# A fused two-layer kernel: 77 context rows without padding in the first attention, and its transposes in pairs

## The reference, cut to what matters

```
xn = layernorm(x)
c2s = softmax((xn Wq_c + bq_c)(ctx Wk_s + bk_s)^T / 16) (ctx Wv_s + bv_s)      # [B, 1024, 256]
s2c = softmax((ctx Wq_s + bq_s)(xn Wk_c + bk_c)^T / 16) (xn Wv_c + bv_c)       # [B,   77, 256]
s2c = interpolate 77 rows linearly to 1024
gate = sigmoid([c2s, s2c] Wg^T + bg)
x = x + tanh(g) * (gate * c2s + (1 - gate) * s2c)
```

## Time and profile before

| | |
|---|---|
| time of three runs | 1067.16, 1067.27, 1069.19 us; median 1067.27 |
| the profiled execution | 1068.09 us, of which the span from first to last instruction is 1066.3 |
| PE busy | 1019.4 us, 96% of the span |
| DVE, ACT, POOL busy | 506.3, 478.4, 305.4 us |
| mean granted clock of PE | 0.986 of full |
| the chain that ended last | PE 83%, DVE 7%, ACT 5% |
| most of the span | MLP products at L1022, 55% of the chain |

### The profile page before, as it was taken

The page is one execution under the profiler, slowest core; times in us unless marked ns, Lnnn a source line. Parts: engine busy times, 40 slices in busy tenths (PEclk is TensorE's granted clock), DMA queues, the critical chain, the costliest instruction groups (busy, mean ns, idle before and its releaser), DMA issues.

```text
span 1066.3 us, 14394 instructions
## 1 busy us (share of the span) xinstructions
PE 1019.4 (96%) x5218; PEld 828.4 (78%) x5218; DVE 506.3 (47%) x1391; ACT 478.4 (45%) x877; POOL 305.4 (29%) x432
## 2 busy tenths in 40 slices
PE   7989998997999999999999999999999999999996
PEld 4757776766789987887889877878898788788885
DVE  6567766765633362456333625563246345134311
ACT  1345442554545353445544544455445444534431
POOL 0025453321251244223502442235034322112111
PEclk9989999998999999999999999999999999999998
DMA  9930003631376365443664654337546545344440
GB/s 336 376 112 2 1 1 119 200 119 40 110 243 206 131 214 158 127 126 113 227 212 138 198 158 137 121 114 233 201 151 197 160 125 158 102 136 153 144 138 23
DMA packets 44276, 158.93 MB, mean 149 GB/s; under 512 B 6448, under 2 KB 6832, under 8 KB 43306
## 3 DMA queue, kind: packets, MB, share of 16 engines
q0 software_dynamic: 29952, 104.88, 31.8%
q1 hardware_dynamic: 10826, 40.63, 11.1%
q10 hardware_dynamic: 3424, 12.45, 3.0%
HBM read 138.01 MB, written 29.36 MB: 157 GB/s over the span
## 4 chain that ended last, share of the span: by engine, by line
PE 83%; DVE 7%; ACT 5%; issue 2%; POOL 1%; DMA 0%; DVEq 0%; POOLq 0%; ACTq 0%
PE psum L1022 55%; PE psum L918 3%; PE psum L822 2%; PE psum L1094 2%; PE psum L1096 2%; PE psum L1095 2%; PE psum L1070 1%; PE psum L832 1%; PE psum L704 1%; PE psum L680 1%; PE psum L944 1%; PE psum L926 1%; PE psum L718 1%; PE psum L734 1%; PE psum L1048 1%
## 5 line engine op out<-in xcount | busy, mean ns | idle before, releaser
L2249 POOL DMA_DIRECT2D mlp_pieces<-in_mlp x176 | 96.5, 556 | 432.9 <-PE psum L1022 429.4
L1022 PE MATMUL psum<-hidden_a_high,mlp_pieces 128*128 128x512 f32 x512 | 205.7, 402 | 0.0
L1022 PE MATMUL psum<-hidden_b_high,mlp_pieces 128*128 128x512 f32 x512 | 202.9, 396 | 0.0
L1022 PE MATMUL psum<-hidden_b_low,mlp_pieces 128*128 128x512 f32 x512 | 199.6, 390 | 0.0
L1022 PE MATMUL psum<-hidden_a_low,mlp_pieces 128*128 128x512 f32 x512 | 199.6, 390 | 0.0
L2095 DVE TENSOR_TENSOR hidden_a_low<-hidden_a,hidden_a_high 128x512 fp32r<-128x512 f32 x128 | 88.2, 689 | 174.0 <-ACT hidden_a_high L1484 173.1
L2095 DVE TENSOR_TENSOR hidden_b_low<-hidden_b,hidden_b_high 128x512 fp32r<-128x512 f32 x64 | 44.4, 693 | 169.4 <-ACT hidden_b_high L1484 169.4
L1022 PEld LDWEIGHTS psum<-hidden_a_high,mlp_pieces 128*128 128x128 f32 x512 | 96.1, 188 | 23.5 <-issue 2.8
L1501 ACT ACTIVATE hidden_a<-psum,mlp_scales 128x512 f32<-128x512 f32 x64 | 44.1, 689 | 154.4 <-PE psum L1022 154.4
L1022 PEld LDWEIGHTS psum<-hidden_a_low,mlp_pieces 128*128 128x128 f32 x512 | 96.2, 188 | 21.7 <-issue 2.6
L1022 PEld LDWEIGHTS psum<-hidden_b_high,mlp_pieces 128*128 128x128 f32 x512 | 96.2, 188 | 20.2 <-issue 0.8
(11 more groups left out here) (290 smaller groups left out, 1825.4 us busy)
## 6 DMA issues: line engine op xcount, KB each, us to landing
mlp_pieces<-in_mlp POOLq DMA_DIRECT2D x176, 512.0 KB, 4.0
slots<-in_zeros SPq DMA_DIRECT2D x3, 3072.0 KB, 37.0
yrows<-expert_rows ACTq DMA_DIRECT2D x18, 512.0 KB, 3.1
mlp_piece_to_examine<-in_mlp SPq DMA_DIRECT2D x16, 512.0 KB, 4.4
slot_rows<-slots SPq DMA_DIRECT2D x15, 512.0 KB, 4.6
x_residual<-in_x SPq DMA_DIRECT2D x4, 1024.0 KB, 23.4
out<-x_residual SPq DMA_DIRECT2D x8, 512.0 KB, 3.4
expert_in<-in_Wi SPq DMA_DIRECT2D x1, 2048.0 KB, 15.6
```

The source lines that it names most:

```text
L1022: last = mm(o, a, b, start=(k == 0 and i == 0), stop=(k == n_k - 1 and i == len(parts) - 1))
L2249: pool.dma_start(mlp_ring[:, r % RING, :], d["mlp"][r % NCHECK]).then_inc(ring_in[r % RING], 16)
```

## The change

Three things. First, `LP` is gone: the arrays have L = 77 partitions, each of the mixing's products contracts over 77 rows, all seven memsets and every wait on `zero_ready` are removed (so is POOL's wait for the last expert product). Second, the transposes of the next batch are issued as pairs of tiles in more places: before the loop after experts 5 and 6; in the loop one pair before `a_sub2char`, one after it, one after `a_sum(5)`, one after `a_sum(6)`. ACT's copies are placed to match, ahead of or behind its own `a_sub2char` copy; DVE's `a_start` is cut in two, with `a_sub2char` between the halves. Third, `kept_context` moves from behind expert 7 to behind expert 2 in DVE's list.

The declaration of VVl below stands for nine such ones.

```diff
-LP = 96
...
-        VVl = place("weights", "values_and_gate_low", [LP, B, 2 * D], F32R)
+        VVl = place("weights", "values_and_gate_low", [L, B, 2 * D], F32R)
...
@@ PE, a_sum
-                mm(ps[:, first, :], P1Th[:, t], VVh[:, b, :], start=True, stop=False)
+                mm(ps[:, first, :], P1Th[0:L, t], VVh[0:L, b, :], start=True, stop=False)
...
@@ PE
             for e in range(5, E):
                 expert(e)
-            a_turn(1, range(JT))
+                if e < E - 1:
+                    a_turn(1, (2 * e - 10, 2 * e - 9))
+            a_turn(1, range(4, JT))
             a_probs_T(0)
             pe.wait_ge(ex_l, E)
             pe.wait_ge(it_r, 1)
-            pe.wait_ge(zero_ready, 7)
...
                 a_sum(c - 1, 4)
+                if c < B - 1:
+                    a_turn(c + 1, (0, 1))
+                else:
+                    b_turn(0, 0, (0, 1))
                 a_sub2char(c)
+                if c < B - 1:
+                    a_turn(c + 1, (2, 3))
                 a_sum(c - 1, 5)
                 if c < B - 1:
-                    a_turn(c + 1, range(0, 4))
+                    a_turn(c + 1, (4, 5))
                 else:
-                    b_turn(0, 0, (0, 1))
+                    b_turn(0, 0, (2, 3))
                 a_sum(c - 1, 6)
                 if c < B - 1:
-                    a_turn(c + 1, range(4, JT))
-                else:
-                    b_turn(0, 0, (2, 3))
+                    a_turn(c + 1, (6, 7))
                 a_sum(c - 1, 7)
@@ ACT
-            act.wait_ge(zero_ready, 7)
+                if e < E - 1:
+                    a_turn(1, (2 * e - 10, 2 * e - 9))
+            a_turn(1, (4, 5))
+            a_turn(1, (6, 7))
             a_sub2char(0)
-            a_turn(1, range(JT))
             a_probs_T(0)
@@ DVE
-            for e in range(2, 5):
+            expert(2)
+            kept_context()
+            for e in range(3, 5):
                 expert(e)
+            a_start(1, range(4))
             a_sub2char(0)
-            a_start(1)
+            a_start(1, range(4, JT))
             for e in range(5, E):
                 expert(e)
-            kept_context()
...
@@ DVE, loop
                 if c < B - 1:
-                    a_start(c + 1)
+                    a_start(c + 1, range(4))
                 else:
                     dve.wait_ge(r2_ps, 2 * B)
                     b_norm(0, 0, range(G))
                 a_sum(c - 1, 4)
                 a_sub2char(c)
+                if c < B - 1:
+                    a_start(c + 1, range(4, JT))
+                else:
+                    b_low(0, 0, (0, 1))
                 a_measure(c - 1, (2,))
                 a_sub2char_low(c)
                 a_sum(c - 1, 5)
-                if c == B - 1:
-                    b_low(0, 0, (0, 1))
@@ POOL
-            pool.wait_ge(ex_ps, E)
             pool.wait_ge(inv_1, 2)
-            pool.wait_ge(zero_ready, 3)
-            for t in (P1Th, P1Tl, SSh, SSl):
-                pool.memset(t[64:LP].bitcast(F32), 0.0).then_inc(zero_ready, 1)
-            pool.wait_ge(zero_ready, 7)
```

More of the change, by code:

```diff
@@ L123, in program @@
         flag = place("small", "weights_not_short", [1, 1])
[L124 removed]
+        yk = place("small", "context_kept", [L, B, D + 1])
         yTb = place("small", "context_projected_of_batch", [P, KC, L])
@@ L774, in a_sum @@
                 first, second = sum_banks(b, j)
[L775 to L781 removed]
+                mm(ps[:, first, :], P1Th[0:L, t], VVh[0:L, b, :], start=True, stop=False)
+                mm(ps[:, first, :], P1Th[0:L, t], VVl[0:L, b, :], start=False, stop=False)
+                mm(ps[:, first, :], P1Tl[0:L, t], VVh[0:L, b, :], start=False, stop=False)
+                mm(ps[:, first, D:2 * D], IT[0:L, t], SSh[0:L, b % 2, D:2 * D], start=False, stop=False)
+                mm(ps[:, first, D:2 * D], IT[0:L, t], SSl[0:L, b % 2, D:2 * D], start=False, stop=True)
+                mm(ps[:, second, 0:D], IT[0:L, t], SSh[0:L, b % 2, 0:D], start=True, stop=False)
+                mm(ps[:, second, 0:D], IT[0:L, t], SSl[0:L, b % 2, 0:D], start=False, stop=True).then_inc(fin, 1)
             def b_turn(g, s, tiles):
@@ L1342, in _ @@
                 a_sum(c - 1, 4)
+                if c < B - 1:
+                    a_turn(c + 1, (0, 1))
+                else:
+                    b_high(0, 0, (0, 1))
                 a_sub2char(c)
+                if c < B - 1:
+                    a_turn(c + 1, (2, 3))
                 a_sum(c - 1, 5)
                 if c < B - 1:
-                    a_turn(c + 1, range(0, 4))
+                    a_turn(c + 1, (4, 5))
                 else:
-                    b_high(0, 0, (0, 1))
+                    b_high(0, 0, (2, 3))
                 a_normalise_probs(c, 1)
@@ L1351, in _ @@
                 if c < B - 1:
-                    a_turn(c + 1, range(4, JT))
-                else:
-                    b_high(0, 0, (2, 3))
+                    a_turn(c + 1, (6, 7))
                 a_sum(c - 1, 7)
@@ L1583, in _ @@
             st.mark(dve.tensor_copy(oner[:], onef[:]))
-            dve.memset(VVh[64:LP].bitcast(F32), 0.0).then_inc(zero_ready, 1)
-            dve.memset(yk[64:LP], 0.0).then_inc(zero_ready, 1)
             dve.wait_ge(cols_in, N_COLS)
@@ L1638, in values @@
                 dve.wait_ge(val_ps, b + 1)
-                if b == 0:
-                    dve.memset(VVl[64:LP].bitcast(F32), 0.0).then_inc(zero_ready, 1)
                 if b >= 2:
@@ L1663, in expert, with a_start @@
                                   wexp_h[:, :, e * D:(e + 1) * D].bitcast(F32), ALU.subtract).then_inc(ex_l, 1)
-            def a_start(c):
-                dve.wait_ge(inv_1, c + 1)
-                if c:
-                    dve.wait_ge(r2_ps, 2 * c)
-                for j in range(JT):
+            def a_start(c, tiles):
+                if tiles[0] == 0:
+                    dve.wait_ge(inv_1, c + 1)
+                    if c:
+                        dve.wait_ge(r2_ps, 2 * c)
+                for j in tiles:
                     normalise(c * JT + j, xn[:, j, :])
@@ L1773, in _ @@
             score_maps()
-            a_start(0)
+            a_start(0, range(JT))
             projected(2, VT, "bv_s", 2)
@@ L2318, in interpolation @@
     w = (pos - lo.astype(np.float32)).astype(np.float32)
-    m = np.zeros((LP, S), np.float32)
+    m = np.zeros((L, S), np.float32)
     np.add.at(m, (lo, np.arange(S)), 1 - w)
     np.add.at(m, (hi, np.arange(S)), w)
-    return np.ascontiguousarray(m.reshape(LP, P, JT).transpose(0, 2, 1).reshape(LP, S))
+    return np.ascontiguousarray(m.reshape(L, P, JT).transpose(0, 2, 1).reshape(L, S))
 def kernel(**inputs):
```

25 lines of the change are left out of this document (7 added, 18 removed).

## The result

| | before | after |
|---|---|---|
| median of timed runs | 1068.23 us (4 runs, 1067.16 to 1069.34) | 1056.53 us (4 runs, 1056.30 to 1058.19) |
| span of the profiled execution | 1066.3 us | 1054.6 us |
| mean granted clock | 0.986 | 0.991 |

The ratio is 0.9897, its 95% interval 0.9883 to 0.991: 1.0% faster. 1054.2 had been forecast, range 1051.5 to 1059.0.

A forecast was written before the change was run, and what follows sets the result against it. PE was busy 96% of the span, so gains could come only from its standstills and lower clock before 162 us. 7.7 + 1.7 + 3.7 = 13.1 us off 1068.09 gives 1055.0, as median 1054.2; range 1051.5 to 1059.0.

The forecast's parts named there:

- Term A: Before the loop: probabilities' transposes start 5.7 us earlier and full clock behind them gains 2.1; 7.7 us taken.
- Term B: Pass 1: its PE waits of 1.9 us and some 0.5 go, 0.7 come back; gain 1.7 us.
- Term C: Pass 2: from 11.48 to 7.8 us, a gain of 3.7 us, partly the lower clock after the old standstill.
- Pass 3: Last transposes in pass 3 wait for DVE's x_T_low, behind the same sum of DVE work; gain 0.
- rival 3: Given back later: after pass 3 another standstill lowers the clock; only A or half of all stays, 1060.5 us; chance 0.07.
- The rows: Mixing products over 77 instead of 96 rows: no column count changes, early memsets ran while DVE waited; gain 0.
- rival 4: 77 rows cost more than 96 in the mixing's 224 products; at 0.1 us each, 1076 us; chance 0.03.
- Rival 1: Clock falls anyway at the bunched transposes before the loop; A's 2.1 us is not gained, 1056.7 us; chance 0.12.
- Rival 2: DVE becomes what PE waits for, through kept_context and the split a_start; 1058.1 us; chance 0.18.
- Rival 5: Memsets go, but another wait holds the copies and pairs; within 0.2%, 1067 us; chance 0.02.

The follow-up runs named there:

- rows only: Kernel before with only the 77 rows and no memsets or zero_ready waits, its order kept: 1061.36 us against 1068.19 us of the kernel before.
- order only: Changed kernel's order, but with 96 rows, seven memsets and their waits: 1054.36 us; repeated, 1055.31 us against 1058.30 us of the changed kernel.
- normalising early: Changed kernel with DVE normalising tiles 4 and 5 of the next batch ahead of sub2char in passes 1 and 2: 1057.63 us against 1058.30 us.
- masking late: Changed kernel with kept_context back behind expert 7 on DVE: 1055.38 us against 1058.29 us of the changed kernel.
- both early: Changed kernel with tiles 4 and 5 normalised before sub2char and DVE's second b_low directly behind the sixth sum: 1055.93 us against 1058.30 us.
- low part early: Changed kernel with DVE's second b_low in pass 3 directly behind the sixth sum, ahead of the seventh: 1054.98 us against 1058.29 us.

## Why the prediction was right, step by step

**Term A** (7.7): measured 80.15 - 72.16 = 8.0. T0 was forecast at 68.0 and came at 67.70; L712 was forecast at 72.4 and came at 72.16; PEclk was 1.00 throughout. The step with a wait of 0.3 for the first pair failed harmlessly: the masking took 2.3 us, not 2.6, and there was none. What the forecast did not say is that A has two covers for one wait. Counted from expert 5 to T0, rows only saves 4.3 us, order only 5.84, both together 5.85; and each alone keeps the clock up. The memsets held the queue, and the order moves the transposes in front of the queue: either is enough for most.

**Term B** (1.7): before, pass 1 takes 9.37 us from the end of `a_sum(4)` to L754 (94.66 to 104.03); 9.37 - 7.67 = 1.7, and undone it came back as 28.35 - 26.64. **Term C** (3.7): 11.48 - 7.91 = 3.6. The size of both held, the mechanism of the wait that remains did not: I had ACT's queue hold the third pair for 0.7 to 0.9 us; it waits 0.4 for DVE's normalising. That pass 2 still took 7.9 us, where 7.8 had been forecast, is luck: two errors cancel. The wait is shorter, and the first pair takes 114.09 - 113.35 = 0.74 us where 0.36 was counted; DVE's four normalisings ahead of it take 2.37 us there, and 1.37 before the loop. The experiment with normalising early shows how near the two are: with DVE's share moved, ACT's queue waits 1.26.

**Pass 3** (0): the step that failed, and with it the sum. L752 came 0.2 us later in relation to T2, as two short waits became one long one of 1.14 us; and the clock fell behind it, 1.6 us more. The prediction took its 0 from DVE's work alone, and said nothing of what a longer standstill does to the clock. Splitting, filling or removing the standstill each took the fall away. That is rival 3 in kind, a given-back part, at 1.8 us of 13.3 instead of half of all; it is why 11.7 came and not 13.1. How near 1054.2 came to 1056.53 says little by itself, since the time to T0 alone varies by 2.1 us between executions of one program. A forecast that costs an edit by its idle time alone misses this.

**The rows** (0): their products cost nothing in either direction (sums are 1.25 us apart, `a_sum(7)` in pass 2, 1.26 in the earlier trace rows), so rival 4 is gone. The wait on the memsets in the new order costs 0.77 us. The whole time does not show it: side by side, order only took 1055.31 us and the changed kernel 1058.30, since the clock did not fall behind pass 3. Once the order is changed, rows without padding are thus worth 0.77 us in the trace, and nothing that the whole time shows.

**Rival 1** did not come: 1.00 from 65 to 75 us, with 8.91 of 10 us busy, in every trace of the new order. But the row that spoke against it, the clock of 1.00 at batch 0's transposes from 20 to 26 us, was one execution. In 7 of the 14 traces of this document, two of the three of the changed kernel among them, the clock fell at that place, between 23 and 25 us; so it could not carry the case against this rival, and that the clock stayed up from 65 to 75 us is known from these traces alone. The Trainium skill, "TensorE: Matmul & The Clock Gate" (Part 4: PE-mode transpose), says that the full clock doesn't engage for transpose mode, which does not count as busy in the same way; by it the rival would have come. From 65 to 75 us the traces disagree; whether these products with the identity run in that mode no row shows. **Rival 2** came as a wait of 0.4 us per pass and not as a bound. **Rival 5** is refuted by the timeline.

**What stays open.** The standstill of 1.1 us in pass 3 brings the fall in all three executions of the changed kernel and with the masking late, and not in both executions of order only and not with normalising early, where PE came to the same place 0.8 to 1.3 us later in relation to T0. So no trace has the fall without the standstill, and the standstill alone is not sufficient. The same holds for the 2.56 us behind pass 3: a fall follows in most kernels, none in order only and both early. What else decides was not found. An effect of the place in time was not tested by itself; T0 2 us later in some executions of the changed kernel did not change the fall. Why the spell at 160 is twice as long in two of the four kernels in which this one was taken away is open too.

## What to carry to other kernels

An engine's in-order queue can hold a wait that belongs to somebody else: here ACT's wait for GpSimd's memsets stopped PE's transposes. Look for what stands ahead of the late instruction on its engine; removing the wait took away 4.3 us here, moving the instruction ahead of it 5.84, and both together 5.85, not the sum. Cut traces at the same events before believing a median: 1.6 us of this one is one spell of lowered clock more or less, and 1.5 us whether a spell lies inside a standstill or behind it. And when idle time is merged into one longer standstill, price the clock behind it.

The best by trace is the changed kernel with the low part early (span 1051.9, T2 to E 2.3 us less); order only came to 1052.2. Side by side, the first's median lies 3.3 us and the second's 3.0 under the changed kernel's. That is little more than the 1.8 us by which its own medians differ, and part of order only's lead is spells that did not come, not work that went away.

## What the runs showed of the hardware

- A standstill of 1.14 us was followed by PE at its lower level (1.2 instead of 2.4 GHz; 0.66 as the mean from 148 to 153 us), at 1.6 us of price; standstills of 1.16 and 2.55 us in nearly the same program (order only) were not.
- The memsets of 32 partitions x 1024 took 0.94 to 1.09 us each on GpSimd, and DVE's narrow operations beside them, L1604 and L1605 of the kernel before, 0.88 instead of 0.17 us: they end at 67.69 and 68.61, each 0.03 us behind a memset. The Trainium skill, "SBUF — State Buffer" (SBUF: two separate sides), calls DVE's and GpSimd's shared port pair an exclusive lock held for the whole instruction; that agrees. It names as partners only some kinds of DVE operation, and whether these two are such no run shows; DVE's own memsets, 0.09 us each, were not held beside a memset of GpSimd in order only (67.82 to 67.99).
